# Flamingo attention kernel: scores of both passes computed in 64-row tiles, one fp16 row as the softmax shift, second-pass query rows brought by DMA

## What is computed

```
scores = einsum('bhqd,bhkd->bhqk', Q, K) / sqrt(8)
if layer == 3: scores = where(mask, -inf, scores)
attn = softmax(scores, axis=-1)          # layer 0 also multiplies by a gate
out  = einsum('bhqk,bhkd->bhqd', attn, V)
x = x + tanh(g_xattn[l]) * (out @ Wo + bo)
```

## Time and profile before

| what | value |
|---|---|
| median of 3 runs | 2006.01 us |
| span of the profiled execution | 2004.8 us |
| TensorE (PE) busy | 92% of the span |
| VectorE (DVE) busy | 71% |
| ScalarE (ACT) busy | 61% |
| DMA, mean rate | 58 GB/s |

### The profile page before, as it was taken

How to read it: one execution, slowest core, us unless ns; L and a number is a source line. 1 busy time by engine, 2 the same in 40 slices (tenths; PEclk the granted TensorE clock), 3 DMA queues, 4 the chain that set the end, 5 groups by cost and what they waited for, 6 DMA issues and landing times.

```text
span 2004.8 us, 43706 instructions
## 1 busy us (share of the span) xinstructions
PE 1839.7 (92%) x14449; PEld 800.7 (40%) x14449; DVE 1427.8 (71%) x2650; ACT 1217.7 (61%) x2194; POOL 146.3 (7%) x239
## 2 busy tenths in 40 slices
PE   6699999977779999997897999999789999999978
PEld 4333333345222333333574233333344444444445
DVE  6688888647878888883685888888457666666448
ACT  3177777742435777775793577777534566565636
POOL 5000000012000000002121000000000000000012
PEclk9899999989998999998898899999988999999979
DMA  9711111105111111110115111111051111111001
GB/s 259 231 36 51 36 52 35 59 1 171 35 44 45 44 44 43 44 35 22 43 54 174 44 45 44 44 44 35 33 174 36 36 35 35 35 35 35 20 6 38
DMA packets 78783, 116.81 MB, mean 58 GB/s; under 512 B 16823, under 2 KB 50958, under 8 KB 78702
## 3 DMA queue, kind: packets, MB, share of 16 engines
q1 hardware_dynamic: 75326, 106.84, 17.9%
q0 software_dynamic: 2432, 7.94, 1.3%
q10 hardware_dynamic: 944, 0.93, 0.1%
HBM read 81.12 MB, written 34.23 MB: 58 GB/s over the span
## 4 chain that ended last, share of the span: by engine, by line
PE 82%; DVE 8%; ACT 3%; DMA 3%; issue 2%; POOL 1%; SPq 1%; DVEq 0%; ACTq 0%; POOLq 0%
PE pv_bank L1420 23%; PE exp_ring L1402 22%; PE score_ring L1389 18%; PE exp_ring L1406 5%; DVE mx L997 3%; PE score_ring L1566 3%; PE exp_ring L1577 3%; DMA k_d<-k2c 2%; PE score_ring L1331 1%; ACT early L771 1%; PE exp_ring L1338 1%; PE score_ring L1479 1%; DMA qp<-ms 1%; DVE stats L913 1%; PE score_ring L1370 1%
## 5 line engine op out<-in xcount | busy, mean ns | idle before, releaser
L771 ACT ACTIVATE early<-exp_ring 128x512 f32<-128x512 f32 (+1 forms) x1728 | 970.7, 596 | 485.1 <-PE exp_ring L1402 303.1
L997 DVE TENSOR_REDUCE mx<-score_ring 128x1 f32<-128x800 f32 (+2 forms) x896 | 784.5, 907 | 163.2 <-PE score_ring L1389 151.2
L1402 PE MATMUL exp_ring<-qp,kp 128*128 128x512 f16 (+1 forms) x1728 | 623.1, 387 | 7.3 <-DMA qp<-ms 6.9
L1389 PE MATMUL score_ring<-kp,qp 128*128 128x400 f16 (+2 forms) x2176 | 573.8, 345 | 43.3 <-DVE mx L997 22.9
L1420 PE MATMUL pv_bank<-early,vg 128*32 128x256 f32 (+1 forms) x6912 | 555.1, 391 | 1.8 <-ACT o_all L760 0.9
L1402 PEld LDWEIGHTS exp_ring<-qp,kp 128*128 128x128 f16 (+1 forms) x1728 | 149.2, 98 | 397.1 <-ACT early L771 279.8
L1389 PEld LDWEIGHTS score_ring<-kp,qp 128*128 128x128 f16 x2176 | 208.8, 99 | 238.8 <-DVE mx L997 86.0
L1420 PEld LDWEIGHTS pv_bank<-early,vg 128*32 128x32 f32 (+1 forms) x6912 | 139.2, 108 | 270.3 <-issue 157.8
L1406 PE MATMUL exp_ring<-mask_eye,mask 128*128 128x256 f16 (+1 forms) x832 | 159.2, 273 | 0.0
L1406 PEld LDWEIGHTS exp_ring<-mask_eye,mask 128*128 128x128 f16 (+1 forms) x832 | 82.3, 99 | 59.0 <-issue 0.7
L607 POOL COPY vg<-v_all 128x416 f32 (+1 forms) x48 | 25.4, 533 | 1030.6 <-PE pv_bank L1420 983.1
(11 more groups left out here) (231 smaller groups left out, 1162.7 us busy)
## 6 DMA issues: line engine op xcount, KB each, us to landing
kp<-k_d SPq DMA_DIRECT2D x128, 400.2 KB, 3.1
k_d<-k1c SPq DMA_DIRECT2D x32, 400.2 KB, 7.0
ctxT<-ctxT_d SPq DMA_DIRECT2D x12, 800.5 KB, 6.2
k_d<-k2c SPq DMA_DIRECT2D x16, 400.2 KB, 7.6
qp<-q_d SPq DMA_DIRECT2D x320, 12.0 KB
k_d<-v_loc POOLq DMA_DIRECT2D x12, 400.2 KB, 9.2
ctxT_d<-ctxT SPq DMA_DIRECT2D x4, 800.5 KB, 7.4
o_all<-in_ctx SPq DMA_DIRECT2D x4, 768.0 KB
```

The source lines that it names most:

```text
L771: act.activation(pt[g][0:rows_, 2 * h:2 * h + 2, :], bank[0:rows_, :].rearrange("p (i q) -> p i q", q=S), ACT.Exp).then_inc(exped, 1)
L997: dve.tensor_reduce(dst, src, AX.XY, ALU.max).then_inc(score_free, 1)
L1389: ins = pe.matmul(pa[slot][:, z, 0:w], qp1[par][:, i, qt * P:qt * P + P], kp1[par][:, at:at + w], start=True, stop=True)
L1402: ins = pe.matmul(bank[0:rows_, :], kp2[par][:, s * P:s * P + rows_], qp2[par][:, 2 * h:2 * h + 2, :], start=True, stop=True, skip_group_c ...
```

## The change

- The contraction of each score matmul covers 64 partitions, the half in which the two heads `2(i//2)` and `2(i//2)+1` lie, in place of 128. This holds for the pieces (line 1389) and for the fills (line 1402), where pair `h` uses half `h`.
- Without a mask, a piece now holds two heads, `m` of the lower half and `2 + m` of the upper half, with the same 400 or 401 keys, one in each bank; VectorE's reduction gives two columns. With the mask, a piece holds one head as before, and the heads go in the order 0, 2, 1, 3. The cross units keep 16 pieces; the local units have 4 pieces of two banks in place of 8 of one, and `ahead` is 5.
- After a fill of the half `h` the piece's matmul of the other half goes first (`half=1 - h`).
- Minus the maximum is kept as one fp16 value: the small operations become one (two with the mask), the transpose has 4 rows, and the maxima go to `qp2` in two DMAs, one per pair of heads.
- The copy `qp2 <- qp1` is gone. `qp2` is set to zero once at the start by VectorE, and `pass2` brings the query rows in four DMAs. SP waits for `m_ok` in place of `q_kept`.

```
-KM = KQ + 2
+KM = KQ + 1
...
-        return [(0, w + 1, 2), (2 * w + 1, w, 2)]
-    return [(0, nk, 1)]
+        return [(0, w + 1), (w, w + 1), (2 * w + 1, w), (3 * w + 1, w)]
+    return [(0, nk)]
...
-        self.turn, self.ahead = (2, 9) if self.local else (3, 7)
+        self.turn, self.ahead = (2, 5) if self.local else (3, 7)
...
-        self.c = QT * HG * len(self.chunks)
+        self.c = QT * PAIRS * len(self.chunks)
...
+    def step(self, j):
+
+        n = len(self.chunks)
+        if self.mask:
+            qt, c, i = j // (2 * HG), j // HG % 2, (0, 2, 1, 3)[j % HG]
+            return qt, [(i, 2 * c), (i, 2 * c + 1)]
+        qt, c, m = j // (PAIRS * n), j // PAIRS % n, j % PAIRS
+        return qt, [(m, c), (PAIRS + m, c)]
...
             def pass2(r, n, par):
                 sp.dma_start(kp2[par][:, 0:r.nk], k_d[r.index][n]).then_inc(in2[par], 16)
+                for i in range(HG):
+                    sp.dma_start(qp2[par][R * i:R * i + KQ, i, :], q_d[r.layer][n, R * i:R * i + KQ, :]
+                                 ).then_inc(in2[par], 16)
...
-                    sp.dma_start(qp2[par][KQ:KQ + 2, :, :], ms[par][:, :]).then_inc(m_in[par], 16)
+                    for h in range(PAIRS):
+                        lo = 2 * R * h + KQ
+                        sp.dma_start(qp2[par][lo:lo + 1, 2 * h:2 * h + 2, :], ms[par][2 * h:2 * h + 2, :]
+                                     ).then_inc(m_in[par], 16)
...
-                    sp.wait_ge(q_kept, r.u0 + n + 1)
+                    sp.wait_ge(m_ok, r.u0 + n + 1)
...
-            for m in qp1:
+            for m in qp1 + qp2:
                 dve.memset(m[:, :, :], 0.0).then_inc(dconst, 1)
...
-                        dve.tensor_reduce(dst, src, AX.XY, ALU.max).then_inc(score_free, 1)
...
+                        dst = mx[par][:, qt * HG:qt * HG + HG, c].rearrange("p (z m) -> p z m", z=2)[:, :, i]
+                        dve.tensor_reduce(dst, src, AX.X, ALU.max).then_inc(score_free, 1)
...
+                def keep_maxima(n, par, first):
...
+                    if r.mask:
+                        dve.tensor_reduce(nm[par][:, :, :].rearrange("p q i -> p (q i)"), mx[par][:, :, 0:cpt], AX.X,
+                                          ALU.max, negate=True).then_inc(mx_done, 1)
+                        dve.wait_ge(mx_done, n + 1)
+                        dve.tensor_scalar(m16[par][:, :, :], nm[par][:, :, :], -MIN_MAX, None, ALU.min
+                                          ).then_inc(m_ok, 1)
+                    else:
+                        dve.tensor_reduce(m16[par][:, :, :].rearrange("p q i -> p (q i)"), mx[par][:, :, 0:cpt], AX.X,
+                                          ALU.max, negate=True).then_inc(m_ok, 1)
...
-                    if r.local:
-
-                        dve.wait_ge(fill, r.fill0 + (n - 1) * r.fills)
-                    dve.tensor_copy(qp2[par][:, :, :], qp1[par][:, :, :]).then_inc(q_kept, 1)
+                    keep_maxima(n, par, first)
...
-                    lo, w, nb = r.chunks[c]
-                    for z in range(nb):
-                        at = lo + z * (S2 // 4)
-                        ins = pe.matmul(pa[slot][:, z, 0:w], qp1[par][:, i, qt * P:qt * P + P],
-                                        kp1[par][:, at:at + w], start=True, stop=True)
+                    qt, banks = r.step(j)
+                    w = r.chunks[banks[0][1]][1]
+                    for z in (half, 1 - half):
+                        i, c = banks[z]
+                        at, rows_ = r.chunks[c][0], slice(2 * R * (i // 2), 2 * R * (i // 2) + 2 * R)
+                        ins = pe.matmul(pa[slot][:, z, 0:w], qp1[par][rows_, i, qt * P:qt * P + P],
+                                        kp1[par][rows_, at:at + w], start=True, stop=True)
...
-                    ins = pe.matmul(bank[0:rows_, :], kp2[par][:, s * P:s * P + rows_],
-                                    qp2[par][:, 2 * h:2 * h + 2, :], start=True, stop=True, skip_group_check=r.mask)
+                    half = slice(2 * R * h, 2 * R * h + 2 * R)
+                    ins = pe.matmul(bank[0:rows_, :], kp2[par][half, s * P:s * P + rows_],
+                                    qp2[par][half, 2 * h:2 * h + 2, :], start=True, stop=True, skip_group_check=r.mask)
...
-                                    piece(n + d, (par + d) % 2, k)
+                                    piece(n + d, (par + d) % 2, k, half=1 - h)
```

More of the change, by code:

```diff
@@ L212, in flamingo @@
         pt = [m[:, 0, :, :] for m in early_mem]
-        mx = [sb(f"mx_{i}", [P, QT * HG, 2]) for i in range(2)]
+        mx = [sb(f"mx_{i}", [P, QT * HG, 4]) for i in range(2)]
         nm = [sb(f"nm_{i}", [P, QT, HG]) for i in range(2)]
-        nmc = [sb(f"nmc_{i}", [P, QT, HG]) for i in range(2)]
-        m16 = [sb(f"m16_{i}", [P, QT, 2, HG], F16) for i in range(2)]
-        ms = [sb(f"ms_{i}", [2 * HG, S], F16) for i in range(2)]
+        m16 = [sb(f"m16_{i}", [P, QT, HG], F16) for i in range(2)]
+        ms = [sb(f"ms_{i}", [HG, S], F16) for i in range(2)]
         mask01 = sb("mask01", [P, QT, S2], F16)
@@ L322, in flamingo @@
         score, score_free = sem("score"), sem("score_free")
-        q_kept = sem("q_kept")
         mx_done, m_ok = sem("mx_done"), sem("m_ok")
@@ L895, in weights @@
                 dve.tensor_copy(mask01[:, :, :], mask8[:, :, :]).then_inc(prep_v, 1)
-                for c, (lo, w, nb) in enumerate(chunk_cols(S2)):
-                    for z in range(nb):
-                        at = lo + z * (S2 // 4)
-                        dve.tensor_scalar(mask_add[:, :, 2 * c + z, 0:w], mask8[:, :, at:at + w], -BIG, None, ALU.mult
-                                          ).then_inc(prep_v, 1)
+                for c, (lo, w) in enumerate(chunk_cols(S2)):
+                    dve.tensor_scalar(mask_add[:, :, c, 0:w], mask8[:, :, lo:lo + w], -BIG, None, ALU.mult
+                                      ).then_inc(prep_v, 1)
                 dve.wait_ge(prep_v, 11)
@@ L977, in attention @@
             def attention(r):
-                cpt = len(r.chunks)
+                cpt = 2 if r.mask else len(r.chunks)
                 def piece(n, par, k, j, first):
-                    qt, c, i = j // (cpt * HG), j // HG % cpt, j % HG
-                    lo, w, nb = r.chunks[c]
-                    src = pa[r.slot(par, k, first)][:, 0:nb, 0:w]
-                    dst = mx[par][:, qt * HG + i, c:c + 1]
+                    qt, ((i, c), _) = r.step(j)
+                    w = r.chunks[c][1]
+                    src = pa[r.slot(par, k, first)][:, :, 0:w]
                     dve.wait_ge(score, r.use(n, k, first) + 1)
@@ L999, in split_maxima @@
-                def split_maxima(n, par, first):
+                        dst = mx[par][:, qt * HG:qt * HG + HG, c].rearrange("p (z m) -> p z m", z=2)[:, :, i]
+                        dve.tensor_reduce(dst, src, AX.X, ALU.max).then_inc(score_free, 1)
+                def keep_maxima(n, par, first):
                     dve.wait_ge(score_free, FREE_SCORE + r.use(n, r.uses - 1, first) + 1)
[L1001 to L1010, removed]
-                                      ALU.subtract).then_inc(m_ok, 1)
@@ L1024, in unit @@
                             piece(n, par, k, j, first)
-                    split_maxima(n, par, first)
-                    if r.local:
-                        dve.wait_ge(fill, r.fill0 + (n - 1) * r.fills)
-                    dve.tensor_copy(qp2[par][:, :, :], qp1[par][:, :, :]).then_inc(q_kept, 1)
+                    keep_maxima(n, par, first)
                 unit(0, 0, first=True)
@@ L1369, in turn, with piece @@
                     for qt in range(QT):
-                        ins = pe.transpose(pa[slot][:, 0, :].bitcast(F16)[0:2 * HG, qt * P:qt * P + P],
-                                           m16[par][:, qt, :, :].rearrange("p a i -> p (a i)"), ident16[:, :])
+                        ins = pe.transpose(pa[slot][:, 0, :].bitcast(F16)[0:HG, qt * P:qt * P + P],
+                                           m16[par][:, qt, :], ident16[:, :])
                     ins.then_inc(score, 1)
-                def piece(n, par, k, first=False):
+                def piece(n, par, k, first=False, half=0):
                     use, slot = r.use(n, k, first), r.slot(par, k, first)
                     if k == r.turn:
-                        pe.wait_ge(m_ok, 2 * (r.u0 + n))
+                        pe.wait_ge(m_ok, r.u0 + n)
                         turn(1 - par, slot, use)
@@ L1441, in unit @@
                                     d, k = todo[given]
-                                    piece(n + d, (par + d) % 2, k)
+                                    piece(n + d, (par + d) % 2, k, half=1 - h)
                                 elif ahead == "rest" and PAIRS * s + h >= r.fills - r.gap:
-                                    pe.wait_ge(m_ok, 2 * (r.u0 + UNITS))
+                                    pe.wait_ge(m_ok, r.u0 + UNITS)
```

17 lines of the change are left out of this document (6 added, 11 removed).

## The result

The changed kernel takes 1960.93 us (median of 4 runs, 1958.14 to 1963.0), the kernel before 2005.72 beside it. The ratio is 0.9781, 95% interval 0.9767 to 0.9794: 2.2% faster. The prediction was 1888 with a range of 1805 to 1950, so the time lies 11 us above the range. The sign and the order of the parts were right, the sum was not.

A forecast was written before the change was run, and what follows sets the result against it. TensorE was taken to bound four of five runs. From 2006.0 us, 184.5 saved in three cross runs, 57 lost in the masked and 9 in the local run gave 1887.5, stated as 1888; range 1805 to 1950.

The forecast's parts named there:

- What bounds the kernel: Four of five runs are TensorE's alone; less VectorE work gains nothing there until TensorE becomes shorter.
- Pairs of row tiles overlap fully: Cross runs: halves of fills and pieces run together, taking TensorE's unit to 14.2 us, 5.7 less.
- VectorE is late next: Cross runs: VectorE's 15.2 us of work leads, TensorE at 14.2 right behind.
- I take 16.0 per unit: Cross unit falls from 19.94 to 16.0 us, bounds 15.2 and 17.5; 14 full units save 55.2 a run.
- under 5%: Sign that the forecast holds: VectorE idle under 5% in the cross run.
- Units 14 and 15: Last two units of each cross run: unit 14 saves 3.3 us, held by ScalarE at 14.5; unit 15 saves 2.0.
- Maxima hidden: Cross units: the maxima's DMAs land within the 2.4 us or more before the next unit's first fill, hidden, barely.
- a sign of being wrong: The forecast is wrong if the first fill of a cross unit waits for the maxima.
- Masked run: 47 shape changes a unit at 0.095 us, less 0.85 of overlap: +3.6 a unit, +57 us in all.
- Local run: SyncE's queue becomes the bound, 5.9 us a unit against 5.33: +9 us, bounds -6 to +31.
- row changes: Rival, masked run: row changes are free, so it gains 14 us instead of losing 57; 1817 us, chance 0.25.
- rival 2: Cross runs: pairs overlap only in part, units about 17.2 us, 50 us more, 1938 us; chance 0.13.

The follow-up runs named there:

- e3_no_row_tiles: The changed kernel without the row tiles, all score matmuls over 128 rows: 2017.3 us, ratio 1.005 to the kernel before.
- e14_turn2: Changed kernel with masked and local runs at 128 rows, VectorE's local copy, one empty place, and the cross and masked transpose one place earlier: 1840.4 us.
- e1_masked_full: The changed kernel with pieces and fills of the masked run back over 128 rows: 1881.5 us, ratio 0.9368 to the kernel before.
- run 57: Not a run label: words from "the masked run 57 us longer"; that stretch went from 377.6 to 435.0 us in the changed kernel.
- e8_order: Changed kernel with the masked run at 128 rows and, after a fill, the piece's matmul of the same half first: 1881.6 us.

## Why the prediction was wrong, by its steps

- **What bounds the kernel: right.** TensorE alone set the cross runs, and lighter VectorE work alone was worth nothing (e3_no_row_tiles, 19.91 a unit).
- **Pairs of row tiles overlap fully: right.** The sum of 14.2 us for TensorE has 0.88 + 2 x 0.17 = 1.22 for a step with two pieces; the step shown takes 0.66 up to the product and 0.57 for it.
- **VectorE is late next: right in kind, mis-sized.** The step that failed is "I take 16.0 per unit": it measured 16.83. I allowed some 0.7 of idle time over 15.2, and VectorE was idle for 1.5 us a unit (9% of it, where I had named under 5%). The gaps behind the maxima (0.55) and behind the transpose (0.26) were as forecast, the 0.45 at the unit's boundary was not, and smaller waits make up the rest. 0.83 x 39 units are 32 us of the miss. The upper bound of 17.5 held the unit.
- **Units 14 and 15: wrong.** I had 14.5 us for unit 14, and it took 15.50: 3 us of the miss in three runs. I let unit 15 fall by 2.0; it went from 16.25 to 16.12. ScalarE's exponentials in it are 0.55 apart and stand still for 1.8 us while TensorE transposes the heads of the first half, as its timeline shows:

```profile
351.23 5.48 ACT L784 ACTIVATE early<-exp_ring 128x512 f32<-128x512 f32 x10 [0.17 <-PE exp_ring L1407]
358.50 6.56 ACT L784 ACTIVATE early<-exp_ring 128x512 f32<-128x512 f32 x12 [1.78 <-PE exp_ring L1407]
```

  My sum had no term for those transposes. 3 x 1.9 = 6 us of the miss.
- **Maxima hidden: not quite, and it did not matter.** "Hidden, barely" was wrong: the first fill of a cross unit waits for them, which I had named as a sign of being wrong. The wait is some 0.13 us, and e14_turn2, which is rid of it, gains nothing.
- **Masked run: right.** Between its first and last evacuation 54.3 forecast, 57.3 measured, and 29.2 against 29.42 a unit; the 0.095 taken from the change by columns was 0.10. That is 3 us of the miss.
- **Start of the masked run: missing.** Up to the first evacuation the run takes 19.6 us more, where my terms for its first unit have 2.6 (3.6 for the changes of shape, less 1). The other 17 go with a stretch at the low clock that no step had: I counted what a change of shape costs in time and not what the new tiles would do to the clock. e1_masked_full gives the time back.
- **Local run: mis-sized.** +9 forecast, +19.3 measured. SyncE's queue was priced at 5.9 a unit (my own terms add up to 5.8) and 6.48 came: the two maxima DMAs take 0.6 each rather than 0.5, and I had no term for the gap behind them (0.18) and for the one between the two groups of loads (0.35). The low clock, which I did not foresee here either, would have held the unit at 5.65 in any case. My upper bound of 7.5 a unit held.

The misses are 32 + 3 + 6 in the cross runs, 3 + 17 in the masked run and 10 in the local one: 71 of the 73 us from 1888 to the measured time. The range failed because they all have one sign and one of them, the clock, had no place in it. Of the rivals, none is what happened: row changes are not free, pairs overlap wholly, and the measured time, nearest to rival 2's 1938 of all that I had named, came from other terms.

## What to carry to other kernels

Before splitting the array into row tiles, count the passages to matmuls of another shape: pairs of tiles pay where fills and pieces stand together (3.1 us of 19.9 per unit here), and each passage to full-height matmuls takes 0.10 us, which made the masked run 57 us longer. Look at the granted clock of short or slow stretches too: here the new tiles cost another 17 us at the start of one run without one more matmul. When an engine stops being the bound, look at places that were laid out for the old balance (empty places, an order, a copy moved to a queue): one constant was worth some 25 us. Work moved to a DMA queue is priced by the queue's own issues in the shortest loop, not by the engine that it leaves.

## What the runs showed of the hardware

- **Matmuls of two 64-row halves don't all start in program order.** In e8_order a fill starts 0.04 us before a piece matmul that stands ahead of it in the program, and the order written in the program makes next to no difference (16.86 against 16.83 us a unit). The Trainium skill ("TensorE: Matmul & The Clock Gate", The mechanism) says that matmuls start and end in program order, with no reordering; these starts speak against it for two row halves, and the measurement decides.
- **Two 64-row matmuls in different halves overlap fully**: they start 0.01 us apart, with 401 and 512 columns, and each keeps its length (0.34 and 0.39 us).
- **Busy time does not tell the clock.** At 64 rows the granted clock was 0.50, the 1.2 GHz level, with TensorE busy 87% in one local run and 100% over 30 us of the masked run; at 128 rows it was 1.00 and 0.99, at 71% and 100% busy. In the cross runs 64-row pairs ran side by side at 1.00, and so did the later masked run, so 64 rows alone do not hold the clock down. What does is not shown.
- **A change between 64 and 128 rows costs 0.10 us**, as much as one between 128 and 32 columns.
- **Each of the two maxima DMAs costs SyncE 0.6 us to issue**, about as much as the single DMA of eight rows before (0.64).
